# Block turns of the level-0 attention's probabilities: TensorE and PSUM before, VectorE's stream transpose after

## The reference

```
y = einsum('bnd,hde->bhne', x, Wkqv) + bkqv          # k 128, q 128, v 8 per head
A = einsum('bhnd,bhmd->bhnm', q, k) / sqrt(128)
A = softmax(where(tril, A, -inf))                    # 2048 x 2048, causal, 16 heads
sa = einsum('bhnm,bhmd->bnhd', A, v); out = sa @ Wp + bp
```

## Time and profile before

| what | value |
|---|---|
| median of three runs | 2808.73 us |
| the profiled execution, its span | 2804.1 us |
| what lies around the span, by the median | 4.6 us |
| attention stage, first half (33.8 to 376.7) | 342.9 us |
| second half before the scan (376.7 to 766.8) | 390.1 us |
| second half with the scan (766.8 to 1138.7) | 371.9 us |
| last rows (1138.7 to 1160.5) | 21.8 us |
| TensorE busy over the whole span | 2620.9 us, 93% |

### The profile page before, as it was taken

How to read it: one execution, slowest core, us unless ns; L and a number is a source line. 1 busy time by engine, 2 the same in 40 slices (tenths; PEclk the granted TensorE clock), 3 DMA queues, 4 the chain that set the end, 5 groups by cost and what they waited for, 6 DMA issues and landing times. The chain is left out here.

```text
span 2804.1 us, 75305 instructions
## 1 busy us (share of the span) xinstructions
PE 2620.9 (93%) x29942; PEld 1739.0 (62%) x29942; DVE 2279.7 (81%) x2918; ACT 1958.5 (70%) x4022; POOL 1699.9 (61%) x1621
## 2 busy tenths in 40 slices
PE   8999999999999999798998999999999999999997
PEld 5555556565665666565665666666666666666665
DVE  6777765675577777789985889989998999899994
ACT  4455555555666666477776888888888888888884
POOL 1000002000266666577766889989999999899992
PEclk9999999999999999999999999999999999999999
DMA  3000000000011112102012111211221221111111
GB/s 93 1 1 1 1 1 3 1 1 11 4 46 46 46 45 46 38 10 90 14 29 66 30 34 31 62 45 35 59 38 37 40 61 36 28 30 36 29 27 37
DMA packets 139208, 90.35 MB, mean 32 GB/s; under 512 B 65219, under 2 KB 135855, under 8 KB 137327
## 3 DMA queue, kind: packets, MB, share of 16 engines
q1 hardware_dynamic: 138863, 85.54, 12.8%
HBM read 60.61 MB, written 6.03 MB: 24 GB/s over the span
## 5 line engine op out<-in xcount | busy, mean ns | idle before, releaser
L587 PE MATMUL ps<-xnT,qp 128*128 128x512 f32 (+3 forms) x1280 | 525.4, 541 | 17.2 <-ACT prob L814 16.3
L1841 DVE TENSOR_TENSOR rot<-ps,tab 128x2048 f32<-128x2048 f32 x192 | 430.4, 2282 | 61.3 <-ACT sq L1621 34.9
L822 ACT ACTIVATE probT<-ps 128x512 f32<-128x512 f32 (+3 forms) x384 | 207.9, 541 | 351.9 <-PE ps L600 351.8
L814 ACT ACTIVATE prob<-ps,ebias,shift 128x1024 f32<-128x1024 f32 (+7 forms) x384 | 360.4, 955 | 123.9 <-DVE ebias L704 60.3
L587 PEld LDWEIGHTS ps<-xnT,qp 128*128 128x128 f32 x1280 | 231.2, 190 | 272.5 <-issue 227.3
L1352 PE MATMUL ps<-wqk,xcT 128*128 128x512 f32 x768 | 355.7, 605 | 28.5 <-DVE area L1907 23.0
L2028 POOL TENSOR_TENSOR rot<-rot,rn 128x1024 f32<-128x1024 f32 x192 | 370.0, 1948 | 7.5
L1442 PEld LDWEIGHTS ps<-wvo,area 128*128 128x128 f32 x3072 | 353.7, 193 | 26.8 <-issue 20.9
L1442 PE MATMUL ps<-wvo,area 128*128 128x128 f32 x3072 | 360.4, 276 | 3.3 <-ACT area L1670 3.3
L695 DVE TENSOR_REDUCE nmx<-ps 128x1 f32<-128x1024 f32 (+7 forms) x256 | 245.6, 986 | 106.7 <-PE ps L587 91.9
L1663 ACT ACTIVATE ps<-ps,nmxl 128x64 f32<-128x64 f32 x1536 | 322.6, 345 | 3.7 <-DVE nmxl L1821 3.6
(11 more groups left out here) (269 smaller groups left out, 5026.0 us busy)
## 6 DMA issues: line engine op xcount, KB each, us to landing
bc<-bc_scratch SPq DMA_DIRECT2D x128, 128.0 KB, 3.1
area<-bc_scratch SPq DMA_DIRECT2D x128, 128.0 KB, 4.0
wqk<-lwqk_dram SPq DMA_DIRECT2D x6, 1024.0 KB, 7.5
xp<-xc SPq DMA_DIRECT2D x96, 48.0 KB, 3.0
xc<-xs SPq DMA_DIRECT2D x96, 32.0 KB
wvT<-lwvT_dram SPq DMA_DIRECT2D x6, 512.0 KB, 8.5
wo<-lwo_dram SPq DMA_DIRECT2D x6, 512.0 KB, 9.2
xc<-xs SPq DMA_DIRECT2D x96, 31.8 KB
```

What stands on the lines that cost most here:

```text
L587: mm = E.matmul(ps[:, 2 * r + o // 512, 0:w], k.qp[:, group % 2, g % NTH * P:(g % NTH + 1) * P], k.xnT[:, k0 + o:k0 + o + w], start=True, ...
L814: A.activation(k.prob[:, r, 0:nk], ps[:, 2 * r:2 * r + 2, :].rearrange("p a b -> p (a b)")[:, 0:nk], ACT.Exp, bias=k.ebias[:, row % 2:row ...
L1841: V.tensor_tensor(k.rot[:, n % 2, w, :, :].rearrange("p c (h d) -> p c h d", d=DH), bcast(heads(what, n), 1, 2), bcast(k.tab[:, n % FRAME, ...
```

## The change

The three inner steps (turn, values, gather) are written anew, and the order with them.

- **Batches.** The work is cut into 48 batches of 8 pieces. A batch is a head's 8 query tiles against one block of 1024 keys. The first half has 16 triangles (pieces of 128 to 1024 keys); the second half has for each head a square (8 pieces of 1024, no mask) and a triangle. The two key blocks of a row are no longer joined by a common maximum: each piece has its own (`mneg`), and GpSimd and ScalarE weigh the two parts against each other later (`part_shares`, `weights`, `combine`).
- **Turns.** TensorE no longer transposes. VectorE turns a whole piece in 32 x 32 blocks with one instruction (`turn_probs`, L756) from `prob` to `probT`, which now holds a whole batch.
- **Values.** They run for a batch at a time, during the next one, in 32 steps of 4 matmuls: 32 keys x 32 columns, up to 256 queries, in the 16 tiles of 32 x 32 of the array (`values`, L702), into banks 4 to 7. Three batches share these banks (a turn of `TURNS`), then ScalarE copies them out, 8 `gather` matmuls sum them up and ScalarE stores the result (17 turns instead of 128 pairs).
- **Value layout.** The weights need 32 keys in each quarter of the partitions. SP writes the values to memory (32 DMAs of 1024 runs of 36 bytes) and reads every batch's back in four copies (192 DMAs), GpSimd spreads them (`vb`).
- **Exponential.** A piece of over 512 keys takes two instructions, one per bank, and TensorE may write the first bank again after the first of them (`prob_first`).
- **Mask.** The causal mask is added by TensorE in the first half too.
- **Fillers.** Queries and experts use the second bank of a short piece's pair; ScalarE takes both out. The gating and sum of the experts go from VectorE to GpSimd. Six of the sixteen expert tiles move to the second half. A visit takes a slot of its own, both banks of a pair: 12 visits instead of 22.
- **The second half** has 128 steps j of two pieces each; taps, scans and visits hang on them. GpSimd's order within a unit of the scan is as before. SP issues the 1 MB load of the first transformer weights at step 46 instead of at the stage's start.
- Several buffers share space with others; that moves no instruction of the transformer.

The diff is long; these are its parts that the sections below speak of.

```diff
+HALF = T // 2 // WIN
+NB = 3 * H0
+BATCH = [(h, 0, 0) for h in range(H0)] + [(h, 1, part) for h in range(H0) for part in range(2)]
+NU = NTH * NB
+FIRST = NTH * H0
+TURNS = [list(range(b, min(b + 3, H0))) for b in range(0, H0, 3)] + [list(range(b, min(b + 3, NB))) for b in range(H0, NB, 3)]
...
+def shares(b):
+
+    return (5, 5, 5, 5, 6, 6) if is_square(b) else (2, 4, 5, 6, 7, 8)
...
+        for h in heads:
+            S.dma_start(k.v_d[h, half].rearrange("c a n -> (c a) n"), k.valL[:, tiles, h, :]).then_inc(s("vd"), 16)
...
+        for c in range(4):
+            S.dma_start(k.staged[WIN * c:WIN * (c + 1), b % 2, :, :], k.v_d[h, part].rearrange("c a n -> a c n")).then_inc(s(f"staged{b % 2}"), 16)
...
+        if i == 2 and b + 2 < NB:
+            if b == 0:
+                S.wait_ge(s("vd"), 16 * H0)
+                save_values(range(H0), 1)
+            elif b == H0 - 1:
+                S.wait_ge(s("vd"), 32 * H0)
+            stage_values(b + 2)
...
+        if what == "piece" and piece(U)[3] > 512:
+            E.wait_ge(s("prob_first"), long_pieces(U))
+        else:
+            pair_free(z)
...
+        for o in range(0, nk, 512):
+            w = min(512, nk - o)
+            if o and z >= 2:
+                pair_free(z - 2)
+            mm = E.matmul(ps[:, r + o // 512, 0:w], k.qp[:, group % 2, i * P:(i + 1) * P], k.xnT[:, k0 + o:k0 + o + w],
...
-        for c in range(min(4, nk // P)):
-            mm = E.transpose(ps[:, 4, c * P:(c + 1) * P], k.prob[:, r, c * P:(c + 1) * P], k.ident[:])
...
+            c, i0 = f % 4, 0 if is_square(b) else f // 4
+            for q in range(4):
+                at = slice(WIN * q, WIN * (q + 1))
+                if i0 == NTH - 1:
+                    o = i0 * STRIDE[x] + WIN * f
+                    of = k.probT[x][at, o:o + WIN]
+                else:
+                    of = k.probT[x][at, 0:NTH * STRIDE[x]].rearrange("p (i n) -> p i n", i=NTH)[:, i0:NTH, WIN * f:WIN * (f + 1)]
+                mm = E.matmul(ps[WIN * c:WIN * (c + 1), 4 + q, WIN * i0:WIN * NTH], k.vb[at, x, NTH * c + f // 4, VB - WIN - VW * j:VB - VW * j], of,
+                              start=j == 0 and f < 4, stop=b in LAST_OF and f >= HALF - 4, skip_group_check=True)
...
+        for i in range(NTH):
+            mm = E.matmul(ps[:, 4, 256 + 3 * VW * i:256 + 3 * VW * (i + 1)], k.oT[:, i, :, :].rearrange("p q n -> p (q n)"), k.pick[:], start=True, stop=True,
...
-        V.tensor_copy(k.probT[:, slot(U), 1, 0:m * P], ps[:, 5, 0:m * P]).then_inc(s("probT1"), 1)
...
+        V.wait_ge(s("prob"), U + 1)
+        if i == 0 and b >= 2:
+            V.wait_ge(s("value_mm"), b - 1)
+        V.transpose(k.probT[x][:, i * STRIDE[x]:i * STRIDE[x] + nk], k.prob[:, U % 2, 0:nk]).then_inc(s("prob_turned"), 1)
...
+        for o in range(0, nk, 512):
+            w = min(512, nk - o)
+            ins = A.activation(k.prob[:, U % 2, o:o + w], ps[:, r + o // 512, 0:w], ACT.Exp, bias=k.mneg[:, U:U + 1], scale=k.unit[:, g, h:h + 1])
+            if o + w < nk:
+                ins.then_inc(s("prob_first"), 1)
+        ins.then_inc(s("prob"), 1)
...
+        A.activation(k.oT.rearrange("p i q n -> p q i n"), ps[:, 4:8, 0:WIN * NTH].rearrange("p q (i n) -> p q i n", n=WIN), ACT.Copy).then_inc(s("ot"), 1)
```

More of the change, by code:

```diff
@@ L371, with is_square, piece, group_of @@
-LONG = [sum(nk > 512 for _, _, nk in PIECES[:U + 1]) for U in range(NU)]
+def is_square(b):
+    return b >= H0 and BATCH[b][2] == 0
+def piece(U):
+    b, i = divmod(U, NTH)
+    h, half, part = BATCH[b]
+    return b, i, part * KB, KB if is_square(b) else (i + 1) * P
+def group_of(b):
+    h, half, part = BATCH[b]
+    return H0 * half + h
+LONG = [sum(piece(V)[3] > 512 for V in range(U + 1)) for U in range(NU)]
 def long_pieces(U):
     return LONG[U]
-def slot(U):
-    row = row_of(U)
-    return 2 * (row % 2) + pieces_of(row).index(U)
@@ L409, with step_of, beside @@
-EXPERT_ORDER = [n for row in range(ROWS) for what, n, half in [filler(row)] if what == "experts" and half]
-def scanned_in(row):
-    u = row - ROWS // 2 - FIRST_SCAN
+def step_of(U):
+    V = U - FIRST
+    return V // 2 if V >= 0 and V % 2 == 0 else None
+SLOTS = []
+for U in range(NU):
+    SLOTS.append(("piece", U, 0))
+    if step_of(U) in VISITS:
+        SLOTS.append(("visit", *VISITS[step_of(U)]))
+SLOT_OF = {U: z for z, (what, U, i) in enumerate(SLOTS) if what == "piece"}
+def beside(U):
+    b, i = divmod(U, NTH)
+    if is_square(b) or i >= 4:
+        return None, 0, 0
+    tile = b if b < 10 else 10 + (b - H0) // 2 if b > H0 and b < H0 + 12 else None
+    if i < 2 and b + 1 < NB:
+        return "queries", group_of(b) + 1, i
+    if i >= 2 and tile is not None:
+        return "experts", tile, i - 2
+    return None, 0, 0
@@ L536, in experts, with first_free @@
[L536 to L543, removed]
+    def first_free(z):
+        what, U, i = SLOTS[z]
+        if what == "piece" and piece(U)[3] > 512:
+            E.wait_ge(s("prob_first"), long_pieces(U))
+        else:
+            pair_free(z)
@@ L638, in attention_pe @@
+    issue(0)
     E.wait_ge(s("raw"), 4)
[L639 removed]
+    issue(1)
     E.wait_ge(s("raw"), 6)
[L641 to L660 removed]
@@ L661, in attention_pe @@
-    values(ROWS - 1)
-    gather(ROWS // 2 - 1)
+    for z, (what, U, i) in enumerate(SLOTS):
+        if what == "piece" and U >= NTH:
+            values(U // NTH - 1, value_steps(U))
+        if z + 2 < len(SLOTS):
+            issue(z + 2)
+        if what == "piece" and U % NTH == NTH - 1 and U // NTH - 1 in LAST_OF:
+            gather(LAST_OF[U // NTH - 1])
+    values(NB - 1, range(HALF))
+    gather(len(TURNS) - 1)
 def attention_dve(k):
     V, s, ps = k.ve, k.sem, k.ps
-    gated = Count()
```

698 lines of the change are left out of this document (357 added, 341 removed).

## The result

The changed kernel takes 2838.2 us (median of four runs, 2825.7 to 2840.5) against 2809.7; the ratio is 1.009, 95% interval 1.007 to 1.011. It is slower, by 0.9%; 2715 was forecast, with a range of 2672 to 2795.

The account below looks back on a forecast made before the run. TensorE was taken to bound the first half and the part before the scan, the scan and GpSimd chain the scan steps. -69 - 40 + 4 + 3 + 8 = -94 on 2804.1 gave 2710, with 4.6 around it 2715; range 2672 to 2795.

Parts of the forecast that it names:

- Value staging: Batch 2's values read back behind 32,768 written packets of 36 bytes at 2.4 ns, landing at 117: TensorE stalls, +8 us.
- rival B: Value staging: small writes cost double, landing at 195, stall 110 us, 2817; 17% for a stall over 30, 7% for the sign.
- First half: First half of the attention: lighter TensorE work, a triangle batch 15.4 us, 17.4 with an expert tile; 274 against 342.9, -69.
- Price of a pass: Value matmuls in 32 x 32 tiles: 16 overlap, 13.8 ns per square pass, 10 per triangle pass; values 5.3 and 4.4 us.
- Rival A: Value matmuls: the 32 x 32 passes overlap only four at a time, making the kernel slower at 2952; chance 8%.
- Before the scan: Second half of the attention before the scan: TensorE's lighter steps, VectorE binding in steps with taps; 350 against 390.1, -40.
- Early rewriting: Rewriting a long piece's first bank early is worth 0, since TensorE finds the banks free in time.
- My loop: Loop over two PSUM pairs: two square pieces take 3.9 us, against 4.8 of TensorE work, so banks are free.
- Rival C: Two-pair loop: VectorE's turn delays the next maximum, a triangle batch takes 17 instead of 15.4 us, total 2768; chance 17%.
- Scan steps: Steps with the scan: VectorE's 6.2 us or the scan and GpSimd chain's 5.5 binds, 5.9 per step as before; +4.
- Ends: End of the attention: TensorE has the last batch's values, copy, gather, store and weighing one after another, about 9 us; +3.

Follow-up runs that it names:

- the first experiment: The changed kernel with only the layout of the stored values altered, so saves write runs of 288 bytes instead of eight of 36: 2757.2 us, ratio 0.981.

## Why the prediction was wrong

**Value staging, +8 forecast, 81 us measured: the step that failed**, and with it the sign. The price was made from the earlier trace rows as time times share: 879 packets, 3 us, 71%, so "at full share 2.4 ns each". For short writes apart from one another that was not too low: they took 1.9 and 1.5 ns. What failed is that no row had writes that adjoin one another; these took 4.1 ns. SyncE began the last 30 of the 32 saves at 42.7 us; at 2.4 ns their 30,720 packets would have landed at about 117, as forecast, and at 4.1 ns they land at about 169. Measured are 171 (195 in rival B). Rival B had nearly the right price and landing, and I gave it 17%, with 7% for the sign; its reason, that small writes as such cost double, is not borne out by the padded ones.

Nor does a rate below full share say what a packet costs. In the first experiment (45 to 48 us) the queue moved 864 packets of 288 bytes in 3 us, 3.5 ns each, but its 40 slices show the DMA engines idle between one save and the next:

```profile
DMA  0028720006940005950002882000784000595000
...
q1 hardware_dynamic: 864, 0.22, 31.7%
```

There SyncE's issue sets the pace, about 0.5 us per DMA of 128 packets.

I also left out two things: the pauses of TensorE beside these writes (12.8 us in value portions, 0.8 in a query), whose cause is not shown, and its clock, which fell while it stood (0.72 between 60 and 191; two passes of a 512-column query matmul took 2.02 instead of 1.08). Of the 80 us the wait is 54.5 and the pauses 13.6; the other 12 are the remainder, which fits the matmuls at the lower clock.

The page "DMA: Bandwidth & Descriptors" of the Trainium skill (Specifications) has transfers under 512 bytes as a read-modify-write. It pointed to the right side. No run here shows such a read, and size alone did not set the price: the same 36-byte runs took 4.1 ns side by side and 1.9 when 64 bytes apart. The 288-byte runs cost no more in the whole kernel than rows of 4,608, but with idle DMA engines they are no test of the page's rule.

**First half, -69 forecast.** Without the stall it takes 292.3, -51. A batch with neither experts nor gather takes 16.9; the forecast's own terms give 14.8 for it (its 15.4 had 0.6 of gather). With experts it is 18.4 against 16.8. Of the 2.1 in the plain batch the masks are 0.6 (1.0 for eight, since six of them cost 0.15 and not 0.05), values 0.5 (4.9 instead of 4.4), scores 0.4, queries 0.3, and 0.3 is a wait for the queries. Of the first batch I had not worked out three waits for the exponential, behind VectorE's gate work at 41 to 51 us, 6 us together; against this the sum had given it values and a gather, 5 us, that it doesn't have. The first of them, in the first experiment:

```profile
43.50 1.95 PE L625 MATMUL ps<-xnT,qp 128*128 128x512 f32 x4 [1.94 <-ACT prob L842]
```

**Price of a pass.** The overlap of 16 tiles was right: a triangle's values in a square batch took 5.34, forecast 4.4; a square's 6.5, forecast 5.3. By the figure of the page "TensorE: Matmul & The Clock Gate" of the Trainium skill (Part 3) 6.9 was estimated (3.5 us of passes times 16 over 10.6, and 1.8 for the portions, are 7.1), nearer than mine either way. Rival A is out. What I missed is the jump: a portion of four steps, which uses each tile once, costs 0.6, one with a fifth step twice that. Dealing the steps by fours gave 26 us back in the first half and before the scan. Why a portion with a fifth step costs twice is not shown.

**Before the scan, -40 forecast; -18.3 measured** (371.8 in the first experiment). Portions are 13 us of the gap of 22, by what portions of four gave back there; scores and masks as above; TensorE also waited 10.9 for the exponential, 3.4 for an expert tile to be copied out and 3.0 for a visit's input.

**Early rewriting, 0 forecast, 19 measured** (7 net of the split). My loop compared mean pieces, 3.9 against 4.8 us. The waits come where a long and a short piece meet: in the first half without early rewriting TensorE waits 0.77 in each batch before the piece of 256 keys, with only the piece of 128 keys between it and the one of 1024 that held its banks. A mean doesn't show that. Rival C did not appear: in the undisturbed first half TensorE was busy 213 of 216 us.

**Scan steps, +4 forecast, +7.7 measured.** They hardly changed, as forecast: 6.0 us each. But the division was wrong: the chain was put at 5.5 us and VectorE at 6.2 in three steps of eight, and with 94 us of VectorE's work gone a step still took 5.84.

**Ends, +3 forecast, +7.0 measured.** The last batch's values took 6.1 us (to 1180.8), not 4.4, and TensorE stood 4.2 us before them:

```profile
1174.66 5.16 PE L702 MATMUL ps<-area,vb 32*32 32x256 f32 x204 [4.17 <-DVE area L756]
...
1186.30 5.95 PE L1441 MATMUL ps<-wqk,area 128*128 128x512 f32 x8 [0.21 <-ACT area L1718]
```

The last line is one of the transformer's first products; the same took 3.70 before, and 5.1 to 6.5 in the other traces of the new attention. It runs behind the idle tail, at a lower clock (0.82 against 0.94 over 54.6 us). That explains some 2 us. I had the transformer unchanged, and it took 7.4 us longer (1651.1). But it varies by more than that in the old attention, whose five traces have 1642.0 to 1651.0 us for it (those of the new one 1643.2 to 1654.3), so the rest of the 7.4 is not shown to come from the change.

## What to carry to other kernels

Price a DMA by its packets and by where they land, and take the rate from a stretch of the same kind of packets in which the DMA engines are full; where they idle between DMAs, the rate is that of the issue. Look at the runs on both sides of a transfer before trusting its bytes: a change of layout took 32,768 packets to 4,096 and was worth more than everything else here. When small matmuls share the array in tiles, try dealing them out in whole rounds of the tiles; it paid here.

## What was not expected of the hardware

- Runs of 36 bytes written side by side: 4.1 ns each over all 16 DMA engines; 64 bytes apart 1.9; 512 bytes apart 1.5.
- The queue's busy share can exceed 100% (139.8%).
- While adjoining short writes fill the DMA engines, other engines pause with no cause in the profile: TensorE's portions of small matmuls by up to 5.7 us, and in the old kernel ScalarE by up to 3.2. Short writes 64 bytes apart, at nearly the same share (130.9%), did none of this. One trace of each.
- In 32 x 32 tiles, 32 passes of 256 columns take 0.6 us, 40 take 1.23, 64 take 1.42.
